# Causal mask inside the decay-exponent products, and the end factors as two 64x64 tiles, in a state-space and feed-forward block

## The reference

```
decay = jnp.exp(dt_t * a)[..., None, None]
b_bar = dt_t[..., None] * b_t
state = decay * state + b_bar[..., None] * x_t[:, :, None, :]
y_t = jnp.einsum('bhn,bhnp->bhp', c_t, state)
```

## Time and profile before

| | us |
|---|---|
| median of 3 runs (lowest, highest) | 1385.83 (1384.98, 1387.1) |
| the profiled execution, its own time | 1388.0 |
| its span, first to last instruction | 1386.3 |
| TensorE busy in the span | 1289.1 (93%) |
| VectorE busy | 1009.5 (73%) |
| ScalarE busy | 746.9 (54%) |
| GpSimd busy | 491.1 (35%) |

### The profile page before, as it was taken

One profiled execution on the slowest core, in us unless ns is written; L12 is line 12 of the kernel. 1 busy time (PEld: TensorE's weight loads), 2 busy tenths in 40 slices (PEclk: granted clock), 3 DMA queues, 4 the chain that ended last, 5 costly groups with the idle time before them and its releaser, 6 DMA issues.

```text
span 1386.3 us, 27618 instructions
## 1 busy us (share of the span) xinstructions
PE 1289.1 (93%) x10544; PEld 813.7 (59%) x10544; DVE 1009.5 (73%) x2362; ACT 746.9 (54%) x1270; POOL 491.1 (35%) x551
## 2 busy tenths in 40 slices
PE   4799999999999999999999999999999999999675
PEld 3364656656475655757566664756557575666543
DVE  4555696877868697776968678686977769685575
ACT  3544584655646476454845556464764548455321
POOL 2030343325351344315433253513443154332533
PEclk9798999999999999999999999999999999999888
DMA  7100000101001010100101010010101000010000
GB/s 208 40 17 1 17 1 1 47 1 47 1 2 47 1 47 1 48 1 17 31 1 47 2 47 1 2 46 2 47 1 47 0 17 16 1 32 1 32 1 31
DMA packets 33378, 32.87 MB, mean 24 GB/s; under 512 B 4952, under 2 KB 31704, under 8 KB 33248
## 3 DMA queue, kind: packets, MB, share of 16 engines
q1 hardware_dynamic: 33248, 31.11, 7.2%
HBM read 22.72 MB, written 8.39 MB: 22 GB/s over the span
## 4 chain that ended last, share of the span: by engine, by line
PE 40%; DVE 24%; issue 15%; POOL 12%; ACT 6%; SPq 2%; DMA 1%; POOLq 0%; DVEq 0%; ACTq 0%
PE bank L1302 23%; PE bank L1466 5%; POOL Cd L709 4%; PE bank L1451 4%; DVE xs L979 4%; POOL y L674 3%; DVE hh L1168 2%; DVE un L954 2%; POOL xdw L704 2%; SPq L560 2%; PE bank L1433 2%; POOL state L720 1%; DVE gn_stats L1092 1%; DVE sh L984 1%; ACT L883 1%
## 5 line engine op out<-in xcount | busy, mean ns | idle before, releaser
L1302 PE MATMUL bank<-sh,WbT 128*128 128x512 f16 x768 | 176.6, 387 | 10.0 <-DVE sh L984 10.0
L1302 PE MATMUL bank<-sh,WcT 128*128 128x512 f16 x768 | 175.6, 379 | 0.0
L893 ACT ACTIVATE mt<-bank 128x512 f32<-128x512 f32 x128 | 69.4, 596 | 186.5 <-PE bank L1373 186.5
L979 DVE SCALAR_TENSOR_TENSOR xs<-xi,taps,xs 128x512 f32<-128x512 f32 x192 | 152.3, 804 | 9.5 <-ACT xs L810 5.0
L704 POOL TENSOR_TENSOR xdw<-xdt,decays 128x512 f32<-128x512 f32 x64 | 66.7, 1042 | 231.6 <-DVE xdt L1060 231.6
L1302 PEld LDWEIGHTS bank<-sh,WbT 128*128 128x128 f16 x768 | 74.2, 99 | 102.0 <-issue 17.4
L1466 PE MATMUL bank<-uh,sign1T 128*128 128x512 f16 x512 | 122.9, 386 | 7.6 <-DVE uh L1157 7.2
L1451 PE MATMUL bank<-WoutT,yT 128*128 128x256 f32 x512 | 117.5, 386 | 12.8 <-POOL yT L688 6.5
L1302 PEld LDWEIGHTS bank<-sh,WcT 128*128 128x128 f16 x768 | 75.1, 98 | 87.0
L921 ACT ACTIVATE hf<-bank,b_col,alpha 128x512 f32<-128x512 f32 x128 | 99.5, 777 | 45.9 <-PE bank L1466 34.2
L1479 PE MATMUL bank<-sign2T,hh 128*128 128x256 f16 x1024 | 119.4, 276 | 1.8 <-DVE hh L1168 1.8
(11 more groups left out here) (181 smaller groups left out, 2540.0 us busy)
## 6 DMA issues: line engine op xcount, KB each, us to landing
xt<-L_attn_input_tensor_dram SPq DMA_DIRECT2D x16, 512.0 KB, 5.1
u<-L_attn_input_tensor_dram SPq DMA_DIRECT2D x16, 512.0 KB, 4.1
out_dram<-u SPq DMA_DIRECT2D x16, 512.0 KB, 2.9
yT<-in_L_ffn_w_dram SPq DMA_DIRECT2D x2, 1024.0 KB, 14.4
BT<-in_L_attn_Wx_dram SPq DMA_DIRECT2D x1, 512.0 KB, 5.1
BT<-in_L_attn_Wz_dram SPq DMA_DIRECT2D x1, 512.0 KB, 6.1
zs<-in_L_attn_Wb_dram SPq DMA_DIRECT2D x1, 512.0 KB, 7.4
zs<-in_L_attn_Wb_dram SPq DMA_DIRECT2D x2, 256.0 KB, 8.0
```

The lines of the kernel that those rows point to most:

```text
L893: nc.scalar.activation(mt[n % 2][:, g].rearrange("p c t -> p (c t)"), bank(t, ("seg", j, q, g))[:, :], ACT.Exp).then_inc(seg_exp.sem, 1)
L979: nc.vector.scalar_tensor_tensor(out=xs[:, c, :], in0=xi[:, c, k:k + BLK], scalar=taps[:, c, k:k + 1], in1=xs[:, c, :], op0=ALU.mult, op1= ...
L1302: mm = nc.tensor.matmul(bank(t, key)[:, :], w[i][:, k, cols(m)], v[h][:, k, :], start=(a == 0), stop=(a == len(terms) - 1))
```

## The change

The mask no longer has a product of its own. Of the 128 contraction rows only 64 depended on the mask-free part that is written per block; now each side g has its own operands, `of_source[g]` and `of_target[g]`. Half of the partitions of each carry the decay sums, and only the rows of that side's heads; the other half carry a unit matrix (in `of_target`) against a triangular mask (in `of_source`), which covers 64 target tokens. So a side is two products, one for each half of the target tokens, of 4x64 = 256 columns, with different weights. TensorE does four products of 256 columns for a chunk where it did four of 512.

VectorE makes the operands with more instructions: `da` and two of `da_wide` instead of one; behind `cum` two that give its partitions their roles (`cum_target`, `cum_source`), then two of `of_target` and two of `of_source` instead of one each.

E leaves `front` and gets a step of its own, `ends`. It is two products in 64x64 tiles (partition halves g), each with 512 columns, and stands behind the carried products of the chunk before (for chunk 0 of a block at the block's start). ScalarE's exp into `Cd` and GpSimd's multiplication of it move with it.

```
-        steps += own(("decays", j), ("front", j, 0)) + tail(("O", j, 0)) + own(("score", j, 0), ("front", j, 1), ("score", j, 1))
-        steps += own(("carry", j, 0)) + tail(("O", j, 1)) + own(("back", j, 0), ("front", j, 2), ("score", j, 2))
-        steps += own(("carry", j, 1), ("back", j, 1)) + tail(("end_stat", j)) + own(("front", j, 3), ("score", j, 3))
-        steps += [(who, "xT", nj, 0)] + own(("carry", j, 2), ("back", j, 2)) + [(who, "xT", nj, 1)]
+        steps += own(("decays", j), ("ends", j, 0), ("front", j, 0)) + tail(("O", j, 0)) + own(("score", j, 0), ("front", j, 1), ("score", j, 1))
+        steps += own(("carry", j, 0), ("ends", j, 1)) + tail(("O", j, 1)) + own(("back", j, 0), ("front", j, 2), ("score", j, 2))
+        steps += own(("carry", j, 1), ("ends", j, 2), ("back", j, 1)) + tail(("end_stat", j)) + own(("front", j, 3), ("score", j, 3))
+        steps += [(who, "xT", nj, 0)] + own(("carry", j, 2), ("ends", j, 3), ("back", j, 2)) + [(who, "xT", nj, 1)]
...
+                nc.vector.tensor_scalar(da[:, :], raw, DECAY_FLOOR, None, ALU.max).then_inc(dt_step.sem, 1)
+                for g in range(HP):
+                    v = of_side(raw, g)[:, None].to_broadcast([P, PARTS, NQ * KI // 2, 2])
+                    nc.vector.tensor_scalar(da_wide[:, g, :, :].rearrange("p m (n f) -> p m n f", f=2), v, DECAY_FLOOR, None,
+                                            ALU.max).then_inc(dt_step.sem, 1)
...
                 dve.wait_ge(*cum_split.count(t, j + 1))
-                dve.wait_ge(*full(s, ("E", sj, NQ - 1)))
-                nc.vector.tensor_tensor(of_target[0:HALF, :, :], cum[0:HALF, None, :].to_broadcast([HALF, KI, P]),
-                                        pair_mask[0:HALF, :, :], ALU.mult).then_inc(ends_made.sem, 1)
-                nc.vector.tensor_tensor(
-                    of_source[HALF:P, :, :, :].rearrange("p q g s -> p (q g) s"),
-                    cum[HALF:P, None, :].to_broadcast([HALF, NQ * HP, P]),
-                    chunk_mask[HALF:P, :, :, :].rearrange("p q g s -> p (q g) s"), ALU.mult).then_inc(ends_made.sem, 1)
+                nc.vector.tensor_scalar(cum_target[:, :], cum[:, :], target[:, 0:1], minus_source[:, 0:1], ALU.mult, ALU.add)\
+                    .then_inc(cum_roles.sem, 1)
+                nc.vector.tensor_scalar(cum_source[:, :], cum[:, :], source[:, 0:1], target[:, 0:1], ALU.mult, ALU.add)\
+                    .then_inc(cum_roles.sem, 1)
+                for need in latest(full(s, ("seg", sj, NQ - 1, HP - 1)), full(s, ("E", sj, NQ - 1))):
+                    dve.wait_ge(*need)
+                dve.wait_ge(*cum_roles.count(t, (j + 1) * 2))
+                for g in range(HP):
+                    rows = rows_of(g)
+                    nc.vector.tensor_tensor(of_target[g][rows, :, :], cum_target[rows, None, :].to_broadcast([HALF, KI, P]),
+                                            pair_mask[rows, :, :], ALU.mult).then_inc(ends_made.sem, 1)
+                for g in range(HP):
+                    rows = rows_of(g)
+                    nc.vector.tensor_tensor(of_source[g][rows, :, :, :],
+                                            cum_source[rows, None, None, :].to_broadcast([HALF, NQ, 2, P]),
+                                            chunk_mask[rows, :, None, :].to_broadcast([HALF, NQ, 2, P]), ALU.mult)\
+                        .then_inc(ends_made.sem, 1)
...
-                    nc.tensor.matmul(bank(t, key)[:, :], ident_h[:, :], past[:, None, :].to_broadcast([P, KI, P]),
-                                     start=True, stop=False)
-                    nc.tensor.matmul(bank(t, key)[:, :], of_source[:, q, g, :],
-                                     of_target[:, :, :].rearrange("p c t -> p (c t)"), start=False, stop=True)\
-                        .then_inc(full_sem(t, key), 1)
+                    for a in range(2):
+                        part = slice(a * HALF, (a + 1) * HALF)
+                        mm = nc.tensor.matmul(bank(t, key)[:, :].rearrange("p (c t) -> p c t", c=KI)[:, :, part],
+                                              of_source[g][:, q, a, :], of_target[g][:, :, part], start=True, stop=True)
+                    mm.then_inc(full_sem(t, key), 1)
...
+            def ends(t, j, q):
+
                 key = ("E", j, q)
+                if q == 0:
+                    pe.wait_ge(*ends_made.count(t, j * 2 * HP + HP))
                 pe.wait_ge(*empty(t, key))
-                nc.tensor.matmul(bank(t, key)[:, :], of_source[0:HALF, q].rearrange("p g s -> p (g s)")[:, HALF:HALF + P],
-                                 of_target[0:HALF, :, :].rearrange("p c t -> p (c t)"), start=True, stop=True)\
-                    .then_inc(full_sem(t, key), 1)
+                for g in range(HP):
+                    rows = rows_of(g)
+                    mm = nc.tensor.matmul(bank(t, key)[rows, :], end_mask[rows, q, :],
+                                          of_target[g][rows, :, :].rearrange("p c t -> p (c t)"), start=True, stop=True)
+                mm.then_inc(full_sem(t, key), 1)
```

More of the change, by code:

```diff
@@ L286, in mamba_sandwich_kernel @@
         cum = sb("cum", [P, P], F16)
-        of_source = sb("of_source", [P, NQ, HP, P], F16)
-        of_target = sb("of_target", [P, KI, P], F16)
+        cum_target = sb("cum_target", [P, P], F16)
+        cum_source = sb("cum_source", [P, P], F16)
+        past = [cum, cum_target, cum_source]
+        of_source = [sb(f"of_source{g}", [P, NQ, 2, P], F16) for g in range(HP)]
+        of_target = [sb(f"of_target{g}", [P, KI, P], F16) for g in range(HP)]
         mt = [sb(f"mt{r}", [P, HP, KI, P]) for r in range(2)]
@@ L342, in uses @@
             if kind == "front":
-                return [*[("seg", *at, g) for g in range(HP)], ("X", *at), ("Bt", *at), ("E", *at)]
+                return [*[("seg", *at, g) for g in range(HP)], ("X", *at), ("Bt", *at)]
+            if kind == "ends":
+                return [("E", *at)]
             if kind == "score":
@@ L1198, in _, with pick @@
             dve.wait_ge(masks_made, MASKS_MADE)
[L1199 to L1207 removed]
+            def pick(dst, pattern, negate=False, axes=AX_XY):
+                nc.vector.tensor_reduce(dst, pattern, axes, ALU.add, negate=negate).then_inc(picks, 1)
+            rows = ident[:, :]
+            roles = rows.rearrange("p (d a m) -> p a d m", d=HP, a=2)
+            pick(of_pair[:, :], rows.rearrange("p (n c) -> p c n", c=KI), axes=AX_X)
+            pick(of_chunk[:, :], rows.rearrange("p (n q c) -> p q n c", q=NQ, c=KI))
+            pick(target[:, :], roles[:, 0])
+            pick(source[:, :], roles[:, 1])
+            pick(minus_source[:, :], roles[:, 1], negate=True)
+            pick(minus_low[:, :], rows.rearrange("p (m i n) -> p i m n", i=2, n=NQ * KI)[:, 1], negate=True)
+            dve.wait_ge(picks, 6)
+            nc.vector.tensor_scalar(of_end[:, :], of_chunk[:, :], target[:, 0:1], None, ALU.mult).then_inc(picks, 1)
             run(first_norm(), 0, handlers)
@@ L1349, in running_sums @@
                 pe.wait_ge(*empty(t, key))
-                nc.tensor.matmul(bank(t, key)[:, 0:P], da_wide[:, :, :].rearrange("p a n -> p (a n)"), upto[:, :],
+                nc.tensor.matmul(bank(t, key)[:, 0:P], da_wide[:, :, :, :].rearrange("p g a n -> p (g a n)"), upto[:, :],
                                  start=True, stop=True).then_inc(full_sem(t, key), 1)
@@ L1366, in front @@
                 if q == 0:
-                    pe.wait_ge(*ends_made.count(t, (j + 1) * 2))
+                    pe.wait_ge(*ends_made.count(t, (j + 1) * 2 * HP))
                 for g in range(HP):
@@ L1484, in _ @@
                 "xT": turn_input, "xi": project_x, "z": project_z, "dt": step_size, "B": project_b, "C": project_c,
-                "cums": running_sums, "sums": decay_sums, "front": front, "score": score, "carry": carry, "back": back, "gn_mean": head_means,
+                "cums": running_sums, "sums": decay_sums, "front": front, "ends": ends, "score": score, "carry": carry, "back": back, "gn_mean": head_means,
                 "Wo": attention_out, "uT": turn_middle, "H": hidden, "O": ffn_out})
```

88 lines of the change are left out of this document (46 added, 42 removed).

## The result

The changed kernel takes 1402.35 us (median of 4 runs, 1399.58 to 1404.35) against 1385.4 us before: 1.0121 times as long, interval 1.0106 to 1.0137. The forecast was 1393.1 us, 7.3 more than before. The sign was right and the time lies in the range, but the loss, 17 us, is more than twice the forecast one. The profiled execution took 1401.36 us (span 1399.6) where that of before took 1388.0 (span 1386.3), so 13.3 us in the span have to be explained.

The account below looks back on a forecast made before the run. TensorE, dense in the chunk stage and already waiting for VectorE's `uh` at the hidden layer, was taken to bound the kernel. Added waits of 25.6 us less 18.3 saved on TensorE gave +7.3: 1393.1 us, range 1380 to 1403.

Parts of the forecast that it names:

- the one that priced the wait: Start of the hidden layer: VectorE's added work between `cum` and `uh` is paid in full as idle TensorE, 14 blocks.
- Seg halves: Chunk's seg stage: four products of 256 columns instead of 512 save 0.41 us x 64 chunks = 26.2 us.
- rival 5: Seg stage: halves save nothing because pieces of 64 columns are slow; 26.2 us more, 1419; chance 3%.
- E out of the front: Between turned B and scores: 0.05 us saved in 50 chunks, 2.5 us; in chunk 0 of 14 blocks 5.6 us.
- The pair: E's two 64x64 tiles behind the carried products: cost 0.25 us x 64 = 16.0 us on TensorE.
- Rival 3: E's pair: its tiles go one after the other; 11.5 us more, 1404.6; chance 9%.
- VectorE's added work: Before `uh`: six instructions for two, 1.65 us later in block 1, 2.0 in block 0; total 25.6 us.
- GpSimd's margin: Moved chain: `Cd` of chunk 3 done about T + 3.0, needed at T + 3.1; hidden by 0.1 us.
- Rival 4: Moved chain (`Cd` of chunk 3, `yT` for X's bank): thin margins become waits; 9.6 us more, 1402.7; chance 8%.

Follow-up runs that it names:

- experiments 8 and 9: `fill_gap2` and `after_again`, run beside each other on the same chip: 1389.22 us and 1400.11 us.
- pad_match: Kernel before, with VectorE writes to an unread spare tile ahead of `uh`, meant to give TensorE a long idle time in both blocks: 1442.28 us.
- fill_gap2: Changed kernel, with unread TensorE products (12 in block 0, 7 in block 1) into a free bank during the wait for `uh`: 1389.22 us.
- late_after: Changed kernel, with VectorE's six factor instructions (roles, `of_target`, `of_source`) moved behind `uh`: 1355.09 us.
- late_before: Kernel before, with VectorE's `of_target` and `of_source` moved behind `uh`: 1378.44 us.
- after_again: The changed kernel once more, unaltered, beside `fill_gap2` on the same chip: 1400.11 us.
- fill_gap: Changed kernel, with unread TensorE products (12 in block 0, 8 in block 1) into a bank that `uh` itself frees, so behind the wait: 1425.89 us.
- pad_both: Kernel before, with five VectorE writes to an unread spare tile between `of_source` and `uh` in both blocks: 1407.52 us.

## Why the prediction missed the size

**The step that failed** is the one that priced the wait: "anything that VectorE does more between `cum` and `uh` is paid in full". It took an idle TensorE to cost its length, and had no term for what an idle stretch does to the work behind it. That term is 10.9 us, in the profiled execution and by experiments 8 and 9 alike, more than the whole forecast change of 7.3.

The trace of before did show it, in a row that I hadn't read. The last batch's feed-forward has no block beside it, and there the kernel before stands still for `uh` as long as the new one does in block 0. The timeline of TensorE and a window, kernel before:
```profile
1328.39 1.65 PE L1312 MATMUL bank<-ident,un 128*128 128x128 f32 x8 [2.17 <-DVE un L954]
1332.61 9.70 PE L1466 MATMUL bank<-uh,sign1T 128*128 128x512 f16 x32 [2.57 <-DVE uh L1157]
...
1332.60:1336.00 3.40, 3.39 (x9) 1.17 (x10) 2.44 (x5) 0.78 (x1) 2.77 (x4) 0.50 0.00 0
```
Behind 2.57 us of idle there are 3.4 us at a clock of 0.50: 9 products go in 3.40 us where 15 or 16 would at 0.217. I had forecast an idle time of 2.8 us for block 0 and 1.8 for block 1. Holding the 2.8 against this row would have given 1.7 us more (half of 3.4) in each of seven blocks, 12 us, and a forecast of some 1405 us. The row isn't quite the same case: shortly before its 2.57 us TensorE had been idle for another 2.17, with 1.65 us of work between them, so it could only warn that such a wait may cost more than its length. `pad_match` and `fill_gap2` show that it does so beside a dense block too.

The other steps, in the order of the prediction:
- **Seg halves**: 0.45 us from seg to X, saving 0.42 us a chunk against 0.41 forecast. Right; rival 5 (no gain from pieces of 64 columns) is out.
- **E out of the front**: 0.10 us a chunk instead of 0.05. **The pair**: 0.80 against 0.60 us, thus 0.20 instead of 0.25. But the forecast took all 64 pairs to stand behind carried products, and the pair of chunk 0 stands alone at the head of the block, where it costs 0.33 us to the next start (463.95 to 464.28) and the 0.09 before it. In sum 48 x 0.20 + 16 x 0.33 + 1.3 = 16.2 us, against 16.0 forecast: close, by two errors that cancel. By the rule of the Trainium skill that the prediction weighed (TensorEngine Tiling (Array Packing), Gotcha 1: PSUM Pressure) it would have been 0.43; the 0.20, and the row that has both products done within 0.38 us (x2 at 482.47), say, as the carried products had, that two diagonal tiles do run together in one bank. Rival 3 is out. The whole saving is 22.4 us instead of 18.3 (`late_after` against `late_before` has 23.4). Of these 4.1 us more, E gives 0.10 x 48 = 4.8 instead of 2.5 and the seg halves 0.6; the last 1.2 are small differences that I haven't divided up.
- **VectorE's added work**: right in kind and close in size, 3.39 and 4.32 us from `cum` to `uh` against 3.2 and about 4; the idle rows show 1.89 and 2.77 against 1.8 and 2.8. The term is 27.7 us instead of 25.6. In block 1 the two roles together take 0.67 us from the start of `cum_target` to `of_target` (446.93 to 447.60 in the trace) against 0.48: that is the error. In block 0 they take 1.25 (530.31 to 531.56) against 0.6, made up for by a second `of_target` and `of_source` that ran mostly without GpSimd beside them (1.26 and 1.44 us for each pair, where one of each took 0.70 and 1.13), and by the two instructions more at `da`, priced at 0.25: `cum` starts 0.14 us ahead of the C products as it did before (0.13).
- **GpSimd's margin**: `Cd` of chunk 3 was not late. The trace has one wait of TensorE for `Cd` in the whole span, 0.8 us. Rival 4 is out.

So the mechanism was in part the forecast one: less TensorE work, paid for with idle time in 14 blocks. Of the 9.7 us between the forecast change of +7.3 and the measured +17, the two terms that it had the size wrong for pull in opposite directions (27.7 - 25.6 = +2.1 and 18.3 - 22.4 = -4.1), and the missing one adds 10.9. That makes 8.9; the rest, 0.8 us, is less than two measurements of the same kernel differ: the terms sum to 27.7 + 10.9 - 22.4 = +16.2, and the repeat, `after_again` against the runs of before beside it, has 1400.11 - 1385.69 = +14.4. That the measured 1402 lies next to the 1402.7 of rival 4 and the 1404.6 of rival 3 is chance: neither happened.

## What to carry to other kernels

Work that makes an operand for later belongs behind the instruction that the busiest engine waits for now: moving the decay factors behind `uh` turned a loss of 17 us into a gain of 30. When an edit makes TensorE wait longer, look in the trace of before for a wait of that length and read the granted clock behind it, since part of the wait may be paid a second time there, 1.4 to 1.7 us a time here. And price a pair of small tiles by its neighbours: behind tiles of its own shape it cost 0.20 us, between tiles of other shapes 0.33 and 0.34.

## What the runs showed of the hardware

- The clock behind an idle stretch, over all runs. Behind 1.21 to 1.90 us of idle before these products none of 42 groups was slow. Behind 2.17 us (`fill_gap`, block 0) 7 of 7 were, behind 2.35 us (`pad_both`) 2 of 7, behind 2.62 us 7 of 7, behind 2.77 us 14 of 14, behind 3.35 us 5 of 7. The order isn't that of the lengths, so the length of this one idle row does not decide it alone; what does beside it was not separated. These are the places beside a dense block. In the first batch two waits of 1.19 and 1.94 us stand close together, and behind them the granted clock is 0.50 until about 126 us in the profile of the kernel after and until about 122 us in that of `after_again`, which is the same kernel.
- The loss is not in proportion to the idle time either. Counted with the products behind the first group, it is 1.35 to 1.74 us in each of the 35 slow places, 1.69 to 1.74 behind 2.17 us of idle and 1.38 to 1.74 behind 3.35. Counted in the first eight products alone it looks like anything from 0.42 to 1.69 us, since the clock can fall late.
- Filling a wait with useless products is worth it where the wait can't be removed: 10.9 us here. Where it can be removed, that is worth four times as much (45.0 us from `after_again` to `late_after`).
- Two products of 64x512 in diagonal 64x64 tiles, into one bank, were both done within 0.38 us, and added 0.20 us behind tiles of their own shape.
- VectorE's instruction on 128 columns with two per-partition scalars took 0.31 to 0.32 us in block 1, and 0.43 and 0.77 in block 0 while GpSimd was at work on `yT` (526.34 to 532.06). No run took GpSimd's work away, so that it is the cause is not shown.
